# A three-layer graph network on one core: a sixth load buffer in the last pass, and a stack loaded later in the second

## What is computed

```python
h = jnp.maximum(_layernorm(x, axis=-1), 0.0)
h = jax.nn.relu(adj @ (h @ W1) + b1)      # x: 2708 x 512, adj: 2708 x 2708, W1: 512 x 1024
h = jax.nn.relu(adj @ (h @ W2) + b2)      # W2: 1024 x 1024
return x + (adj @ (h @ W3) + b3)          # W3: 1024 x 512
```

## Time and profile before

| | us |
|---|---|
| median of 3 runs | 1590.32 (1589.25 to 1590.51) |
| the profiled execution, its own time | 1585.07 |
| its span, first to last instruction | 1583.3 |
| PE busy | 1572.2 (99%) |
| DVE busy | 866.4 (55%) |
| ACT busy | 644.3 (41%) |
| POOL busy | 527.9 (33%) |
| mean granted TensorE clock | 0.999 of full |

### The profile page before, as it was taken

One profiled execution on the slowest core, in us unless ns is written; L12 is line 12 of the kernel. 1 busy time (PEld: TensorE's weight loads), 2 busy tenths in 40 slices (PEclk: granted clock), 3 DMA queues, 4 the chain that ended last, 5 costly groups with the idle time before them and its releaser, 6 DMA issues.

```text
span 1583.3 us, 21103 instructions
## 1 busy us (share of the span) xinstructions
PE 1572.2 (99%) x7638; PEld 1353.4 (85%) x7638; DVE 866.4 (55%) x1360; ACT 644.3 (41%) x1145; POOL 527.9 (33%) x488
## 2 busy tenths in 40 slices
PE   9999999999999999999999999999999999999998
PEld 7888889988878898989898989888898888888898
DVE  8983433255443556353545444864565547666666
ACT  5442222234343423233333333543454446555454
POOL 5864544336665444000000003574202333121302
PEclk9999999999999999999999999999999999999999
DMA  6966657554687888454656567783554458798887
GB/s 241 337 197 235 215 182 222 178 163 151 199 275 243 281 284 283 125 174 117 204 154 217 172 207 233 263 268 115 173 144 110 104 148 268 238 318 269 270 250 225
DMA packets 211091, 334.52 MB, mean 211 GB/s; under 512 B 25608, under 2 KB 96896, under 8 KB 210988
## 3 DMA queue, kind: packets, MB, share of 16 engines
q1 hardware_dynamic: 171484, 239.78, 48.8%
q0 software_dynamic: 15680, 55.31, 10.5%
q10 hardware_dynamic: 23824, 38.10, 6.9%
HBM read 243.75 MB, written 89.36 MB: 210 GB/s over the span
## 4 chain that ended last, share of the span: by engine, by line
PE 91%; DMA 4%; DVE 3%; ACT 1%; ACTq 0%; issue 0%; DVEq 0%; SPq 0%
PE ps L1814 29%; PE ps L1815 29%; PE ps L1816 29%; DVE ring L1445 2%; DMA raw<-adjT 1%; PE ps L1904 1%; PE ps L1903 1%; DMA raw<-HX 1%; DMA raw<-TS 1%; ACT ring L1196 0%; DVE pair_buf L1487 0%; ACT pair_buf L1241 0%; DMA raw<-adjX 0%; PE ps L1852 0%; ACTq L900 0%
## 5 line engine op out<-in xcount | busy, mean ns | idle before, releaser
L1445 DVE TENSOR_TENSOR ring<-raw,ring 128x512 fp32r<-128x512 f32 (+1 forms) x522 | 372.6, 729 | 414.4 <-ACT ring L1196 412.5
L1196 ACT CAST ring<-raw 128x512 fp32r<-128x512 f32 (+1 forms) x564 | 319.5, 576 | 495.2 <-PE ps L1816 350.5
L1814 PE MATMUL ps<-slots,still 128*128 128x512 f32 (+1 forms) x504 | 183.5, 364 | 1.6 <-DVE still L1393 1.1
L1815 PE MATMUL ps<-slots,still 128*128 128x512 f32 (+1 forms) x504 | 183.3, 364 | 0.0
L1816 PE MATMUL ps<-slots,still 128*128 128x512 f32 (+1 forms) x504 | 183.3, 364 | 0.0
L1814 PE MATMUL ps<-ring,even 128*128 128x512 f32 (+1 forms) x480 | 175.4, 365 | 2.1 <-DVE ring L1445 2.1
L1815 PE MATMUL ps<-ring,even 128*128 128x512 f32 (+1 forms) x480 | 175.3, 365 | 0.0
L1816 PE MATMUL ps<-ring,even 128*128 128x512 f32 (+1 forms) x480 | 175.1, 365 | 0.0
L1814 PE MATMUL ps<-ring,S 128*128 128x512 f32 (+1 forms) x420 | 154.2, 367 | 2.6 <-DVE ring L1445 2.4
L1815 PE MATMUL ps<-ring,S 128*128 128x512 f32 (+1 forms) x420 | 152.9, 364 | 0.0
L1816 PE MATMUL ps<-ring,S 128*128 128x512 f32 (+1 forms) x420 | 152.9, 364 | 0.0
(11 more groups left out here) (160 smaller groups left out, 3016.8 us busy)
## 6 DMA issues: line engine op xcount, KB each, us to landing
raw<-TS SPq DMA_DIRECT2D x160, 256.0 KB, 3.2
raw<-adjT SPq DMA_DIRECT2D x122, 256.0 KB, 3.8
raw<-adjT SPq DMA_DIRECT2D x41, 512.0 KB, 4.6
TS<-made SPq DMA_DIRECT2D x20, 1024.0 KB, 6.5
raw<-TS SPq DMA_DIRECT2D x80, 165.0 KB, 2.5
raw<-HS SPq DMA_DIRECT2D x50, 256.0 KB, 2.9
raw<-P SPq DMA_DIRECT2D x44, 256.0 KB, 4.0
HS<-pair_buf POOLq DMA_DIRECT2D x20, 512.0 KB, 4.6
```

Of the source, the lines that this page charges most:

```text
L1196: act.copy(hi, src).then_inc(hi_done, 1)
L1445: dve.tensor_tensor(lo, src, hi.bitcast(F32), ALU.subtract).then_inc(lo_done, 1)
L1814: pe.matmul(out, st_hi, mv_hi, start=start, stop=False)
L1815: pe.matmul(out, st_hi, mv_lo, start=False, stop=False)
```

## The change

In the last pass the raw ring has six buffers in place of five. The sixth is the old third place of `extra3`, so that `extra3` has two. The sixth is put in front of the others: `raw` starts one buffer earlier, the ring runs over buffers 1 to 5 up to the last pass and over 0 to 5 in it. ACT's wait of the stacks of the last pass for the store of `spill_0` (`g_stored[0]`) is taken out; SP waits for it before the first load into buffer 0. The place of a stack in `extra3` is free when the group two before has ended.

In the second pass the list of part 0 gets one more empty entry at its head: the first stack stands behind the seventh tile of the first group and its tail (n = 6) instead of behind the fourth tile (n = 3), and the second stack at n = 18 instead of 16.

```diff
-        self.cuts = self.lows = self.raws = self.slots = self.tails = 0
-        self.raw_user = [None] * RAW
+        self.cuts = self.lows = self.slots = self.tails = 0
+        self.raws, self.first_raw = 1, 1
+        self.raw_user = [None] * (RAW + 1)
...
     def take_raw(self, j, loads):
         j.raw = self.raws
-        before = self.raw_user[j.raw % RAW]
+        before = self.raw_user[j.raw]
         j.raw_freed = before
-        self.raw_user[j.raw % RAW] = j
-        self.raws += 1
+        self.raw_user[j.raw] = j
+        self.raws = self.raws + 1 if self.raws < RAW else self.first_raw
...
             if part == 0:
-                extra = [lambda: None, lambda: load_extra(X11)] + [lambda: None] * 4 + [lambda: load_extra(X12)]
+                extra = [lambda: None] * 2 + [lambda: load_extra(X11)] + [lambda: None] * 4 + [lambda: load_extra(X12)]
...
     def pass3(late):
         at["rotation"] = 2
+        p.first_raw = 0
...
-                        k.part, k.pair = part, n % 3
-                        k.place_freed = ("group", ends[n - 3] if n > 2 else w3_end)
+                        k.part, k.pair = part, n % 2
+                        k.place_freed = ("group", ends[n - 2] if n > 1 else w3_end)
...
-    extra3 = place("extra3", [P, 3, 2, QUARTER], F32R, PAIRS * ROW)
+    extra3 = place("extra3", [P, 2, 2, QUARTER], F32R, PAIRS * ROW)
...
-    raw = place("raw", [P, RAW, BANK], F32, raw_at)
+    raw = place("raw", [P, RAW + 1, BANK], F32, raw_at - BANK * 4)
+    assert raw_at - BANK * 4 == PAIRS * ROW + 2 * 2 * QUARTER * 4
...
                 if j.raw_freed is not None:
                     wait_cut(sp, j.raw_freed)
-                elif r >= RAW - 2:
-                    sp.wait_ge(stage_stored[r - RAW + STAGES], 16 * CHUNKS)
+                elif r == 0:
+                    sp.wait_ge(g_stored[0], plan.stored["g", 0])
+                elif r >= RAW - 1:
+                    sp.wait_ge(stage_stored[r - RAW - 1 + STAGES], 16 * CHUNKS)
...
-                if j.kind == "extra3":
-                    act.wait_ge(g_stored[0], plan.stored["g", 0])
```

More of the change, by code:

```diff
@@ L744, in stage @@
     def stage(s):
-        return (stage_a, stage_b, raw[:, RAW - 2:RAW, :])[s // 3][:, s % 3, :]
+        return (stage_a, stage_b, raw[:, RAW - 1:RAW + 1, :])[s // 3][:, s % 3, :]
     def columns(half, c):
@@ L787, in gcn_kernel @@
         stage_stored = [sem(f"stage_stored{i}") for i in range(STAGES)]
-        raw_in = [sem(f"raw_in{r}") for r in range(RAW)]
+        raw_in = [sem(f"raw_in{r}") for r in range(RAW + 1)]
         hi_done = sem("hi_done")
@@ L837, in cut_tile @@
         def cut_tile(j):
-            src = hold[:, HOLD[j.part], j.pair, :] if j.raw is None else raw[:, j.raw % RAW, :]
+            src = hold[:, HOLD[j.part], j.pair, :] if j.raw is None else raw[:, j.raw, :]
             if j.kind == "s":
@@ L1009, in load @@
                     return
-                r = j.raw % RAW
+                r = j.raw
                 if j.raw_freed is not None:
                     wait_cut(sp, j.raw_freed)
-                elif r >= RAW - 2:
-                    sp.wait_ge(stage_stored[r - RAW + STAGES], 16 * CHUNKS)
+                elif r == 0:
+                    sp.wait_ge(g_stored[0], plan.stored["g", 0])
+                elif r >= RAW - 1:
+                    sp.wait_ge(stage_stored[r - RAW - 1 + STAGES], 16 * CHUNKS)
                 if j.kind == "h1":
@@ L1168, in cut @@
                 else:
-                    act.wait_ge(raw_in[j.raw % RAW], j.raw_count)
+                    act.wait_ge(raw_in[j.raw], j.raw_count)
                 if j.place_freed:
```

## The result

The changed kernel takes 1580.30 us (median of 5 runs, 1580.08 to 1582.09), the kernel before on the same chip 1589.27 (5 runs, 1587.63 to 1590.51). The ratio is 0.9946, 95% interval 0.9934 to 0.9958: 6.7 to 10.5 us faster. The prediction, 1586.0 with a range from 1582.5, had the sign and was too small by half. The two profiles differ by much less than the timed runs: 1585.07 to 1582.09. The first lies 4.2 us under the shortest of the three timed runs it was read beside, the second is the longest of its five.

What follows compares the result with a forecast made beforehand. PE, busy 1572.2 of 1583.3 us, was taken as the bound, losing 5.8 us to late loads in the last pass's narrow chunk. 4.3 us returned, others nothing: 1590.32 - 4.3 = 1586.0 us, range 1582.5 to 1590.3.

Steps and rivals of the forecast that it cites:

- The sixth buffer: Last pass, narrow chunk: one more load in flight returns 4.3 us of 5.8 lost to late loads.
- The wide chunks: Last pass, the two wider chunks before the narrow one: PE shows no wait, nothing lost and nothing to gain.
- The carry-over: Whole kernel: the timed median's 5.25 us above the profiled run, at an unseen place, stays unchanged after the edit.
- The rival that said so: Last pass: timed runs lose more to late loads than the profiled one, so about 1582 us; chance 0.12.
- What is late next: Last pass, narrow chunk: DVE subtractions made long by POOL's additions keep 0.5 us at three places, 1.5 us.
- Loads that share a bound: Last pass: a sixth load lengthens landing from 2.9 to 3.7 us, returning 0 to 2.5 us, 1589.3; chance 0.36.
- The price of the sixth buffer: Last pass: two stack places instead of three make ACT's cast wait, covered by 9.6 us; cost nothing.
- The first stack: Start of second pass: moving it leaves PE's wait for the third tile unchanged; 0 us, from -1 to +2.
- The slower side: Start of second pass: the moved stack comes late, PE stands and its clock falls, 1593.5 us; chance 0.06.

Runs made afterwards that it cites:

- e3: The kernel before, unchanged, measured and profiled once more: 1589.83 us, ratio to before 1.0001.
- e1: The kernel before with only the move of the second pass's stack, five raw buffers throughout: 1589.43 us, ratio to before 0.9997.
- e11: The kernel before, five buffers, with the steps of the last block of layer one two cuts later: 1587.64 us, ratio to before 0.9992.
- e10: The changed kernel, unedited, measured again: 1581.45 us, ratio to before 0.9955.
- e2: The changed kernel with the second pass's stack back behind the fourth tile, so the sixth buffer alone: 1581.77 us, ratio to before 0.9952.
- e5: The changed kernel with the steps of the last block of layer one two cuts later: 1579.97 us, ratio to before 0.9944.
- e12: The same kernel as e5, measured again: 1578.32 us, ratio to before 0.9945.
- e7: The changed kernel, six buffers, with POOL's additions in the last pass's narrow chunk cut to one column: 1580.49 us, ratio to before 0.9945.
- e4: The changed kernel with the raw ring cut to four buffers in the last pass: 1615.25 us, ratio to before 1.0162.
- e8: The kernel before, five buffers, with POOL's additions in the last pass's narrow chunk cut to one column: 1587.29 us, ratio to before 0.9992.
- e9: The changed kernel with six buffers only from the last pass's third chunk on, five in its wide chunks: 1583.76 us, ratio to before 0.9967.
- e6: The kernel before, five buffers, with moving-tile loads in the last pass's narrow chunk cut to half the columns: 1583.40 us, ratio to before 0.9969.

## Why the prediction was right in its mechanism and wrong in its size

**The sixth buffer.** The mechanism is as predicted: loads ended last, the round of 4.0 us for five buffers was too tight, six free it, ACT then waits for PE. What failed is the term of the sum: "7 x 9.60 is 67.2. So 5.8 us are lost there", and with it "take 4.3 us as returned". It was read from one execution. Over the four profiles with five buffers and untouched loads and additions (before, e3, e1, e11) the narrow part takes 74.9 us on average, over the five with six (the change, e10, e2, e5, e12) 69.2: 5.7 us returned.

**The wide chunks.** "The first chunks ... lose nothing today and can gain nothing" failed too. They take 204.2 us on average in those four profiles and 202.9 in every one with six: 1.3 us. Together 7.0 us, inside the 6.7 to 10.5 of the timed result and beside the 7.2 of e10 and 7.6 of e2. Of the 9.0 between the two medians 2.0 are then without a place in the profiles; they are within that interval.

**The carry-over.** "The median of the runs is 1590.32, 5.25 us above the profiled run, at a place I can't see; I carry the difference over." That was the choice that cost the range. A profile 4.2 us under the shortest of the three timed runs and 5.25 under their median is an execution with fewer of the losses that vary, and the larger part of the losses that vary were ones the change removes. The rival that said so had 0.12, and its mechanism was the true one. Some 3 us of the 5.25 were in this place: the last pass took 5.9 us more in e3 than in that profile, (76.67 + 205.24) - (73.02 + 202.99), and 3.1 us more in the mean of the four. With the 7.0 in place of the 4.3 the forecast would have been 1583.3 us, inside its own range and still 3 us over the result. Three of the four profiled executions (e3, e1, e11) are themselves among the timed runs; that the other timed runs are like them is an inference, since they left no traces.

**What is late next.** The right cause and about the right size, in part by luck. What six buffers leave over 67.2 us is 1.6 to 2.5 us. By e7 the additions of POOL are 0.7 to 1.6 us of it, in the fourth and seventh groups (the rows have them at 1567 us as well, which the prediction passed over). The rest is mostly that some groups take 9.81 us and not 9.60, a term that the sum didn't have.

**Loads that share a bound.** Half true: landing of TS went from 2.9 to 3.3 us (3.0 to 3.3 over the seven profiles with six buffers), not to the 3.7 that would have cancelled the gain, and the DMA share went to 0.83 at 251 GB/s. The rule of the Trainium skill in "DMA: Bandwidth & Descriptors", "Latency and other measured facts", that access takes longer under load, agrees in sign with e4, e3 and the change (2.6, 2.9 and 3.3 us), though e5 with six buffers has 3.0, as e1 has with five; it gives no figure for one load more in flight, and the runs do.

**The price of the sixth buffer.** Nothing, as predicted: with two places for the stacks the wide part is at its shortest.

**The first stack.** Zero, as predicted, and for the reason given: the wait at 445 us is the third tile's and stayed. The slower side didn't show. The new wait of 0.38 us at 439.91 is of the second tile; ACT's chain there ran 0.5 us later than before from 425 us on, ahead of anything that the change moves, and no other profile has it.

## What to carry to other kernels

Where a profiled run is faster than every timed run, look for what varies before carrying the difference over: profile the old kernel once or twice more and take the mean of the disputed stretch. A ring of load buffers needs a round (landing, conversion, release) below buffers times pace with room for the slow landings, not at the median; here 4.0 us against 4.0 lost 6 to 12 us over the last pass (against 202.9 + 67.2), and with one buffer of 2 KB a partition more 1.6 to 2.5 are left. Moving work away from a tile that is not the late one gains nothing until the late one is mended: ask which tile PE waits for, and what stands before that tile in the order.

## What the runs showed of the hardware that I had not expected

A narrow group without a wait takes 9.60 us in some places and 9.81 in others (64 matmuls, 0.150 or 0.153 us apart in the mean), at a full granted clock. In the change's second narrow group, of 9.60 us, half of the starts are 147 ns apart and half 153; in its fifth, of 9.81, all are 153 or 154. In e7 the seven take 9.93, 9.82, 9.81, 9.81, 9.82, 9.81 and 9.82. No run tells what decides it.

PE's standstill at the start of the second pass is followed by half clock for about 3.4 us in some profiles and not in others. Take as gap the time from one matmul's start to the next, less the 0.227 us of undisturbed ones. It was so after gaps of 2.29 us (before), 2.28 (the change, e8), 2.15 (e4), 2.12 (e9) and 2.01 (e6). It was not after 2.29 in e3, nor after 1.90 (e7), 1.87 (e2), 1.51 (e10) and 1.25 (e1). So one length of gap went with half clock in one execution of a kernel and not in another. In e4 two waits of the last pass, 2.1 us up to 1565.42 and 2.7 us up to 1603.06, went with a clock of 0.50 too (windows of 1565.4 to 1568.7 and of 1603.0 to 1606.2). At half clock for 3.4 us each, I estimate that some 3 of its 35 us are an effect of the clock. The window of e3, with a clock of 1.00 over all of it:

```profile
442.00:460.00 18.00, 15.88 (x70) 12.86 (x69) 9.37 (x11) 8.32 (x15) 11.05 (x11) 1.00 0.88 299
```
